# A graph network's four layer normalisations: the reciprocal root made by GpSimd instead of ScalarE

## What is computed

```
def _layernorm(x, axis=-1, eps=1e-05):
    m = jnp.mean(x, axis=axis, keepdims=True)
    v = jnp.var(x, axis=axis, keepdims=True)
    return (x - m) / jnp.sqrt(v + eps)

h = jnp.maximum(_layernorm(x, axis=-1), 0.0)
x = x + _L0_gnn_ref(h, adj, ...)     # attention over neighbours, 4 heads
h = jnp.maximum(_layernorm(x, axis=-1), 0.0)
x = x + _L1_gnn_ref(h, adj, ...)     # ((1+eps) h + adj h) W1, relu, W2
h = jnp.maximum(_layernorm(x, axis=-1), 0.0)
x = x + _L2_gnn_ref(h, adj, ...)     # adj (h W)
h = jnp.maximum(_layernorm(x, axis=-1), 0.0)
x = x + _L3_gnn_ref(h, adj, ...)     # five steps of a gated recurrent unit
```

## Time and profile before

| | us |
|---|---|
| median of 3 runs | 734.93 |
| lowest and highest run | 733.04, 737.34 |
| profiled execution, its time | 732.92 |
| profiled execution, its span | 731.1 |
| TensorE busy | 666.5 (91%) |
| VectorE busy | 645.2 (88%) |
| ScalarE busy | 536.7 (73%) |
| GpSimd busy | 407.9 (56%) |

### The profile page before, as it was taken

The page is one execution under the profiler, slowest core; times in us unless marked ns, Lnnn a source line. Parts: engine busy times, 40 slices in busy tenths (PEclk is TensorE's granted clock), DMA queues, the critical chain, the costliest instruction groups (busy, mean ns, idle before and its releaser), DMA issues.

```text
span 731.1 us, 15079 instructions
## 1 busy us (share of the span) xinstructions
PE 666.5 (91%) x4380; PEld 430.8 (59%) x4380; DVE 645.2 (88%) x1425; ACT 536.7 (73%) x978; POOL 407.9 (56%) x356
## 2 busy tenths in 40 slices
PE   2788999999999999985599999999999999999994
PEld 1467788777778777774255555445454544544542
DVE  3788899999999999872399999999999999999995
ACT  0375888888888888873288878777787777877774
POOL 2354666666666666652155555555565555655553
PEclk9998999999999999998599999999999999999997
DMA  5011110001010000000233333333333333333332
GB/s 140 10 30 30 30 31 29 29 29 29 29 29 29 29 29 14 0 2 0 43 56 60 57 57 61 73 72 72 72 68 72 72 72 72 60 72 72 72 72 59
DMA packets 114647, 35.26 MB, mean 48 GB/s; under 512 B 87680, under 2 KB 114624, under 8 KB 114624
## 3 DMA queue, kind: packets, MB, share of 16 engines
q1 hardware_dynamic: 114624, 34.98, 22.3%
HBM read 9.80 MB, written 4.19 MB: 19 GB/s over the span
## 4 chain that ended last, share of the span: by engine, by line
DVE 25%; issue 13%; PE 9%; ACT 2%; DVEq 1%; DMA 0%; POOLq 0%; POOL 0%; ACTq 0%; SPq 0%
DVE h_parts L1271 10%; PE psum L50 9%; DVE cand L1278 5%; DVE new L1267 4%; DVE r L1282 3%; DVE t_parts L1263 2%; DVE out L1254 1%; PE psum L1157 1%; ACT final L1195 1%; ACT z L1207 1%; DMA h_nodes<-h_parts 0%; ACT zc L1209 0%; DVE h_parts L1273 0%; ACT cand L1212 0%; DVEq L1254 0%
## 5 line engine op out<-in xcount | busy, mean ns | idle before, releaser
L50 PE MATMUL psum<-h_parts,gru_w 128*128 128x512 f16 x720 | 183.5, 382 | 2.4 <-DVE h_parts L1273 2.4
L1238 POOL TENSOR_TENSOR h0T<-cand,zh 128x512 f32 (+1 forms) x80 | 101.8, 1272 | 143.6 <-DVE cand L1278 143.6
L50 PE MATMUL psum<-t_parts,gru_w 128*128 128x512 f16 x720 | 181.5, 379 | 0.0
L50 PEld LDWEIGHTS psum<-h_parts,gru_w 128*128 128x128 f16 x720 | 69.8, 98 | 86.2 <-issue 5.2
L1232 POOL TENSOR_TENSOR zh<-z,h0T 128x512 f32<-128x512 f32 x80 | 101.9, 1273 | 29.1 <-ACT z L1207 29.0
L50 PEld LDWEIGHTS psum<-t_parts,gru_w 128*128 (+1 forms) x720 | 66.7, 98 | 67.0 <-issue 8.7
L1271 DVE CAST h_parts<-h0T 128x512 f16 (+1 forms) x80 | 95.3, 1191 | 4.9 <-PEq L361 4.8
L1204 ACT CAST t_parts<-psum 128x512 f16<-128x512 f32 x80 | 46.9, 586 | 66.4 <-PE psum L50 66.4
L554 POOL TENSOR_TENSOR prob<-prob,row_max 128x512 f32<-128x512 f32 x64 | 67.8, 1071 | 48.6 <-DVE row_max L919 48.6
L1212 ACT ACTIVATE cand<-new,gates_b 128x512 f32<-128x512 f32 x80 | 65.1, 813 | 5.4 <-DVE new L1267 1.9
L1207 ACT ACTIVATE z<-psum,gates_b 128x512 f32<-128x512 f32 x80 | 62.3, 778 | 5.7 <-PE psum L50 0.7
(11 more groups left out here) (133 smaller groups left out, 1266.3 us busy)
## 6 DMA issues: line engine op xcount, KB each, us to landing
x_all<-in_x SPq DMA_DIRECT2D x16, 256.0 KB, 3.2
adj<-in_adj SPq DMA_DIRECT2D x16, 256.0 KB, 2.9
out_x<-out SPq DMA_DIRECT2D x16, 256.0 KB, 2.3
h_nodes<-h_parts SPq DMA_TRANSPOSE x80, 3.1
gw<-in_L_gnn_weight SPq DMA_DIRECT2D x1, 320.0 KB, 5.7
W<-in_L_gnn_W SPq DMA_DIRECT2D x2, 128.0 KB, 5.6
wi<-in_L_gnn_w_ih SPq DMA_DIRECT2D x1, 192.0 KB, 5.9
wh<-in_L_gnn_w_hh SPq DMA_DIRECT2D x1, 192.0 KB, 5.8
```

Of the source, the lines that this page charges most:

```text
L50: return nc.tensor.matmul(out, lhsT, rhs, start=start, stop=stop)
L1238: pool.tensor_tensor(state(now), by_graph(cand[now.s][:, :]), by_graph(zh[now.s][:, :]), ALU.add)\
```

## The change

`rstd_of` moves from ScalarE to GpSimd. There it is an addition of eps to the variance (TENSOR_TENSOR, 128 x 4), a wait for that addition, and a power (TENSOR_TENSOR with the operation pow, 128 x 4, the exponent -0.5 in a tile of its own). Eps and the exponent are held in constant tiles of 128 x 4, set by two memsets ahead of the pipeline. The four calls also get new places: for normalisations 0 and 3 between the centring and the multiplication of `normalise`; for normalisation 1 behind the whole of normalisation 0; for normalisation 2 at the end of the slot, behind normalisation 3. ScalarE loses the eight instructions of each slot and gets nothing for them. VectorE, TensorE and SyncE keep their instructions and their order.

```diff
@@ GpSimd
+            def rstd_of(group, n):
+
+                pool.wait_ge(var_ready[n], group.count)
+                if group.before(1).exists:
+                    pool.wait_ge(y_ready[n], group.before(1).count)
+                pool.tensor_tensor(eps_var[n][:, :], mean_var[n][:, :, 1], eps_tile[:, :], ALU.add)\
+                    .then_inc(eps_added[n], 1)
+                pool.wait_ge(eps_added[n], group.count)
+                pool.tensor_tensor(rstd[n][:, :], eps_var[n][:, :], half_tile[:, :], ALU.pow).then_inc(rstd_ready[n], 1)
+
...
                 pool.tensor_tensor(y[n][:, :, :], xs(group), mean_var[n][:, :, 0:1].to_broadcast([128, GROUP, DIM]),
                                    ALU.subtract).then_inc(centred[n], 1)
+                rstd_of(group, n)
                 pool.wait_ge(rstd_ready[n], group.count)
                 pool.wait_ge(centred[n], group.count)
...
                 if at(0):
                     normalise(at(0), 0)
+                if at(2):
+                    rstd_of(at(2), 1)
                 if at(1):
                     less_max(at(1), 0)
...
                 if at(3):
                     normalise(at(3), 3)
-
-            pool.memset(eps_col[:, :], EPS).then_inc(constants, 1)
+                if at(2):
+                    rstd_of(at(2), 2)
+
+            pool.memset(eps_tile[:, :], EPS).then_inc(constants, 1)
+            pool.memset(half_tile[:, :], -0.5).then_inc(constants, 1)
@@ ScalarE
-            def rstd_of(group, n):
-
-                act.wait_ge(var_ready[n], group.count)
-                a.activation(log_var[n][:, :], mean_var[n][:, :, 1], ACT.Ln, bias=eps_col[:, 0:1])\
-                    .then_inc(log_done[n], 1)
-                act.wait_ge(log_done[n], group.count)
-                a.activation(rstd[n][:, :], log_var[n][:, :], ACT.Exp, scale=-0.5).then_inc(rstd_ready[n], 1)
...
-                if at(0):
-                    rstd_of(at(0), 0)
...
-                if at(2):
-                    rstd_of(at(2), 1)
...
-                if at(3):
-                    rstd_of(at(3), 3)
...
-                    rstd_of(at(2), 2)
                     normalise(at(2), 2)
```

More of the change, by code:

```diff
@@ L374, in first_layers @@
         mean_var = [one(f"mean_var{n}", [128, GROUP, 2]) for n in LAYERS]
-        log_var = [one(f"log_var{n}", [128, GROUP]) for n in LAYERS]
+        eps_var = [one(f"eps_var{n}", [128, GROUP]) for n in LAYERS]
         rstd = [one(f"rstd{n}", [128, GROUP]) for n in LAYERS]
@@ L392, in first_layers @@
         hid = one("hid", [128, 2, COLS])
-        eps_col = one("eps_col", [128, 1])
+        eps_tile = one("eps_tile", [128, GROUP])
+        half_tile = one("half_tile", [128, GROUP])
         x_loaded = [sem(f"x_loaded{s}") for s in range(2)]
@@ L401, in first_layers @@
         var_ready = [sem(f"var_ready{n}") for n in LAYERS]
-        log_done = [sem(f"log_done{n}") for n in LAYERS]
+        eps_added = [sem(f"eps_added{n}") for n in LAYERS]
         rstd_ready = [sem(f"rstd_ready{n}") for n in LAYERS]
@@ L587, in slot @@
                     normalise(at(3), 3)
-            pool.memset(eps_col[:, :], EPS).then_inc(constants, 1)
+                if at(2):
+                    rstd_of(at(2), 2)
+            pool.memset(eps_tile[:, :], EPS).then_inc(constants, 1)
+            pool.memset(half_tile[:, :], -0.5).then_inc(constants, 1)
             for s in range(2):
                 pool.memset(hW[s][:, :, :, HEAD_DIM:], 1.0).then_inc(constants, 1)
-            pool.wait_ge(constants, 3)
+            pool.wait_ge(constants, 4)
             pool.wait_ge(gru.loaded, gru.all_loaded)
@@ L742, in slot @@
                     turn_y3(at(3))
-            pe.wait_ge(constants, 3)
+            pe.wait_ge(constants, 4)
             slots(pe, slot)
@@ L866, in _ @@
             act.preload_act_table_set("natural_log_exp_and_others")
-            act.wait_ge(constants, 3)
+            act.wait_ge(constants, 4)
             act.wait_ge(gru.loaded, gru.all_loaded)
```

## The result

The changed kernel takes 804.73 us, the median of four runs (802.21 to 807.12), against 734.19 (733.04 to 737.34) for the kernel before on the same chip. The ratio is 1.0953, 95% interval 1.0895 to 1.1011. The profiled execution took 806.98 us, its span is 805.2, and TensorE's granted clock is 0.943 over it, against 0.976 before. The forecast was 758 us, with a range up to 788: the direction was right, the size was not. One thing is needed for the small ratios further down: single runs of the kernel before spread from 731.3 to 739.4 us in this study, so a ratio within some 0.5% of 1 hangs on where its runs of before fell.

A forecast was written before the change was run, and what follows sets the result against it. VectorE's instruction list was taken to bound the 18.6 us loop slot. Twelve slots losing 1.84 us (22.1) plus 2 outside made 24, giving 757 on the profiled 732.9 or 759 on the median: forecast 758 us, range 744 to 788.

The forecast's parts named there:

- VectorE's list sets the pace: Loop slot: VectorE waits for no other engine, so its instructions and self-waits make the 18.6 us; TensorE 0.6 behind.
- both shifts become late: VectorE's two shifts per loop slot wait for GpSimd's rstd; the losses add up to 0.64 + 3p us.
- the price p of the power: Length of GpSimd's 128 x 4 power, shown by no row; bounds 0.10 and 1.04 us, taken as 0.4.
- the prediction's own formula: Loss per loop slot: 0.64 + 3p us, 1.84 at p = 0.4; from p = 0.6 on, p - 0.6 more.
- shift 2 late, and its length: VectorE's shift of normalisation 2 loses 0.16 + p us, ending behind `add_self`; normalisation 3 adds p - 0.6 from p = 0.6.
- shift 1 late: VectorE's shift of normalisation 1, behind GpSimd's normalisation 0 and two pairs of addition and power, loses 0.48 + 2p us.
- pair of normalisation 0 alone: GpSimd's addition and power between centring and multiplication of normalisation 0 start that multiplication 0.24 + p us later.
- TensorE waits longer for y: Sign expected in the profile after: TensorE's waits for ScalarE's y grow; no size given.
- Outside the loop: Slots before and after the 12 loop slots: slot 3, the emptying pipeline and first normalisations, estimated at 2 us lost.
- The power is dear: Rival: GpSimd's power exceeds 1.04 us; at p = 2, 8.0 us a slot, 97 in all, some 830; chance 0.10.
- VectorE gets ahead of `add_self`: Rival: shift 2 starts first and escapes its 0.66 us stall; 738 at p = 0.15, 746 at 0.4; chance 0.07.
- ScalarE is the pacer: Rival: ScalarE sets the loop's pace, so removing its work helps; 728 at best, more likely 731; chance 0.06.

The follow-up runs named there:

- with the clock held: The changed kernel with twelve and five unused matmuls ahead of TensorE's two waits for y, those waits moved behind the bank users' waits: 794.63 us, ratio 1.0815.
- the kernel with the cheap operation: The changed kernel with a multiplication in place of the power, order and waits kept, output not the reference's: 742.46 us, ratio 1.0100.

## Why the prediction was right, and where it was wrong

**VectorE's list sets the pace, and both shifts become late: right.** In the kernel after VectorE's new waits in the loop are the two for `rstd` and, where TensorE's clock falls, longer ones for ScalarE's `e_parts` and scores. Each half alone costs about what the chain says (+1.18 and +1.23 a slot).

**The step that failed is a term of the sum, the price p of the power.** "I take p = 0.4, near that and a little above the geometric middle of the bounds": it measured 1.015, just inside the upper bound of 1.04. I had no row for it, and leaned on ScalarE's 0.50 for the same function, which is another engine's way of making it. The nearest row of GpSimd itself, 1.04, was the bound that I took to be far. The rest of the mechanism holds when p is put right. With p = 1.015 the prediction's own formula gives 0.64 + 3.05 + 0.42 = 4.10 us a slot; with the clock held it measured 3.96. By parts:

| term | by the formula at p = 1.015 | measured, clock held |
|---|---|---|
| shift 2 late, and its length | 0.16 + 1.015 + 0.42 = 1.59 | 1.26 + 0.40 = 1.66 |
| shift 1 late | 0.48 + 2.03 = 2.51 | 2.44 |
| pair of normalisation 0 alone | 0.24 + 1.015 = 1.26 | 3.96 - 2.69 = 1.27 |

The first two measured terms are those of the slot shown and add up to 4.10; the wait at shift 2 is 1.26 in one slot and 1.13 in the next, and the mean of the two explains half of the 0.14 by which they exceed 3.96. Two details of these were off and nearly cancel. The addition takes 0.20, not 0.15, but the power starts 0.08 behind it, not 0.15 (of which the prediction's sums use 0.14). And shift 2 waits only 0.82 in the kernel after itself: the late `e_parts` moves the variance back, so that GpSimd is free and waits for it (1.09 us). In the slot shown of that kernel VectorE loses 0.82 + 0.40 + 2.44, 1.40 at `e_parts` and 0.16 at the scores, 5.22 in all; its marks are 23.79 apart, 5.18 more than 18.61.

**TensorE's clock was not in the sum at all.** The prediction says "TensorE waits longer for y", and gives that no price. The wait of 2.64 us is followed by a stretch at half clock, and this costs 23.57 - 22.57 = 1.0 us a slot on average, about 12 of the 74 us between the two profiled executions. The experiment with the filling matmuls shows it: the same kernel, 10 us shorter in all, by more work on the engine that waits. The slot at full clock in the kernel after, 22.53 us, says the same without any change of code. With only normalisation 1 moved it is there in some slots, with only normalisation 2 moved it is not.

**Outside the loop: 2 us forecast, 14.7 measured.** VectorE waits 5.5 us for `rstd`, in four waits, between 20 and 94 us, where it had no wait for `rstd` before. The sentence that the loss in slot 3 is covered by VectorE's wait for ScalarE does not hold at this price. I did not take the rest apart: with the clock held, the loss outside the loop is as large (62.6 us at the recurrent unit's first product, 12 x 3.96 = 47.5 of them in the loop), so most of it is not the clock.

**Why even the range was too short.** Its upper end had p nearly right (1.04) and gave 4.2 us a slot, 50 in the loop. It lacked the clock, 12, and 12 more outside the loop; with both it would have been 812, against the 804.7 measured. Of what the forecast itself was short by, some 50 us against the profiled executions, the price p is the largest part: 12 x (4.10 - 1.84) = 27. The clock is 12 and the slots outside the loop are 13.

**The rivals.** The power is dear was the nearest: its mark, a second instruction of the pair over 1 us ahead of what follows it, is what the trace shows, but p stayed under the 1.04 from which that rival was to begin, and p = 2 was too much. VectorE gets ahead of `add_self` did not come about; 0.07 us in the order of two starts decided it, and the kernel with the cheap operation shows both outcomes in turn. ScalarE is the pacer: not so. No row shows a gain from its 128 removed instructions, and its waits for the shift grew to 59.1 us.

**The order of starts decides who stands still.** In the pairs of rows shown here a shift that starts behind a 512-column operation of GpSimd ends 0.01 to 0.03 us behind it (after 0.82 to 1.22 us), and the one that starts ahead of it takes 0.16. SBUF — State Buffer of the Trainium skill, section Who interferes with whom, says that the first of the two to issue gets the shared pair of ports and the other is fully blocked; the trace agrees as far as the shift goes, with 0.16 against 1.20 in neighbouring slots of one run. That GpSimd is blocked in turn this pair does not show, since there `add_self` starts 0.02 us after the shift has ended.

## What to carry to other kernels

Price an unknown operation by the rows of the engine that will run it, not by what another engine needs for the same function, and when no row exists let the bounds, not their middle, decide how sure the forecast is. When a change makes a busy TensorE wait for longer than it did, the wait may be paid twice, the second time as a stretch at half clock; filling matmuls in the wait are a cheap way to find out. Before moving a long GpSimd operation away from a short VectorE one, look for the short one that it lands on.

## What the runs showed of the hardware

- From 4 columns on, GpSimd's power costs 0.36 us and 0.16 for each column of 128 numbers (1.01 us for 4 columns, 5.43 for 32; one column takes 0.56), its addition 0.19 to 0.25 for the same shapes.
- A GpSimd addition of 128 x 4 takes 0.20 us, and the instruction that waits for it starts 0.08 behind its end, where it was 0.15 behind an operation of 512 columns.
- A pause of 0.21 us on GpSimd's queue is enough to turn a shift of 1.20 us into one of 0.16.
- TensorE is granted 0.50 of its clock behind waits of 1.90 and 2.64 us in these rows, but kept 1.00 behind other waits of 1.90 and 2.64 in the same two runs, and behind one of 1.81. So the length of one such wait does not decide it, and what does stays open. In the slot shown of the kernel after, the clock falls when the matmuls have begun again (1.00 in the window of the wait, 0.88 in the next, 0.50 in the one after); in the kernel after with `add_self` moved it is 0.50 already in a window of the wait, 198 to 200 us.
